# GpSimd's slot scatters of a two-layer attention and experts kernel, moved behind the transposed scores

## The chip, the cores and the metric

The kernel runs on one core of a Trainium2 chip, as one program. A core has four engines that compute, each with its own stream of instructions: TensorE (PE, matrix multiplication), VectorE (DVE), ScalarE (ACT) and GpSimd (POOL), and a fifth, SyncE (SP), that issues DMA transfers. They meet through semaphores alone. The metric is device time in microseconds, the median of several executions. It stands a few microseconds above the span of a profiled execution, which runs from the first to the last instruction.

## The reference

Two layers, each a cross attention and a mixture of eight experts of which every token uses two, on 32 batches of 128 tokens with 256 features. The change lies in the first attention and in what prepares the first experts:

```python
x = x + _L0_xattn_ref(_layernorm(x), ctx_1024, ctx_1024, itok_BxS2_0_31, mask_BxS2_ff1, ...)
    # q = norm(x) @ Wq.T, k = ctx @ Wk.T, v = ctx @ Wv.T, 16 heads of 16
    scores = jnp.einsum('bhqd,bhkd->bhqk', q, k)
    lm = layer_indices[:, :, None] == layer_indices[:, None, :]
    scores = jnp.where(lm, scores + am, NEG)
    attn = jax.nn.softmax(scores, axis=-1)
    ctx = jnp.einsum('bhqk,bhkd->bhqd', attn, v)
    return ctx @ Wo.T + bo
x = x + _L0_ffn_ref(_layernorm(x), router_w, w1, w2, expert_scale)
    logits = xf @ router_w.T
    top_w, top_idx = jax.lax.top_k(jax.nn.softmax(logits), 2)
    # every token goes through its two experts
x = x + _L1_xattn_ref(_layernorm(x), ctx_1024, ...)
x = x + _L1_ffn_ref(_layernorm(x), ...)
```

The kernel computes the experts for the tokens that chose them. So each token gets two slots in a list sorted by expert, and its number is written ("scattered") to these slots in a table in DRAM, from which the experts' stage later reads which rows to gather.

## The kernel before

The program is a row of stages, and each engine runs its part of each stage in order: the first attention (`a_...`), the first experts (`b_...`), the second attention (`c_...`), the second experts (`d_...`). Within a stage nothing is scheduled by a tool. Every engine has one loop over the iterations b, written out by hand, and a block of 128 tokens passes through it over several iterations; `inside(b)` leaves out blocks below 0 and above 31.

In iteration b of the first attention TensorE does, in this order: the scores of block b (L804, tiled matmuls of 32 rows), the values of block b-1 (L843, tiled matmuls of 32 columns), transposes and the term for unseen keys (L932, L863, L872, L852), the router's logits of block b-3 (L941), the transpose of the clamped maxima (L812), the transposed scores (L787, L826 and L830, the last two tiled), the projections of the context of block b+2 (L901, L904), the transpose of `att` (L911), the query projection (L882) and the output projection of block b-1 (L918). VectorE takes the residual and its statistics (L1026 to L1032), the maxima over the scores (L1051), clamps them (`mexp`, L1058), picks experts (L1096, L1098), combines (L1069 to L1076), and for each finished group of blocks makes the slots (L1126 to L1141). ScalarE copies out of PSUM (`oT` L704, `attT` L711 and others) and takes the exponentials (`pT`, L695) of the transposed scores. `st_done[r]`, r from 0 to 3, are the four semaphores that the last transposed scores of a block raise, one for each of four banks of PSUM.

GpSimd's part of an iteration is short. `norm2(b-2)` makes the scale of the second normalisation (L539 to L543, three small instructions that start when VectorE has that block's statistics), `mask(b+1)` compares tokens (L555), `add_bias(b-1)` adds a bias to the residual (L561), and `norm1(b+4)` makes the scale of the first normalisation (L527 to L531). Between them stand the slot scatters. `scatter(b, k)` (L569) is one indirect DMA, which GpSimd issues itself; it writes the numbers of a block's 128 tokens to their slot k, where the slots come from `gsidx`. Two scatters belong to a block. `scattered_at(b, k)` says in which iteration one is issued, and the dictionary `turn` holds the list of each iteration: for the first blocks the two of block b-8 in iteration b, from iteration 8 on, and near the end, where groups get smaller, three in iterations 28 and 29 and four in 30, 31 and 32, then two in each. The first scatter of a group waits for `slot_ready`. When the loop is over, GpSimd waits until all have landed and goes on to the first experts, whose first gathers read the table.

## Time and profile before

| what | us |
| --- | --- |
| runs of the kernel before | 1456.46, 1464.56, 1462.81 |
| their median | 1462.81 |
| span of the profiled execution | 1453.1 |
| TensorE busy in the span | 1337.7 (92%) |
| GpSimd busy in the span | 680.5 (47%) |

A row of a timeline gives the start in us from the span's start, how long the row lasts, the engine, the line, the operation, output and inputs, and how many instructions it merges; in brackets stands how long the engine was idle before it and what ended that. PE is TensorE, DVE VectorE, ACT ScalarE, POOL GpSimd. The granted clock is TensorE's, 1.00 being 2.4 GHz.

### The profile page before, as it was taken

The numbers are of one execution on the slowest core, as the hardware profiler recorded it, in microseconds if no ns is written. First come the engines' busy times: TensorE is split into PE (matmuls) and PEld (weight loads), VectorE is DVE, ScalarE is ACT, GpSimd is POOL, SyncE is SP. The second block draws the span as 40 slices with busy tenths as digits, with TensorE's granted clock in tenths as the row PEclk, the third lists the DMA queues.
The fourth block names the chain that finished last, engine by engine and source line by source line (L and its number), as shares of the span: only waits on it lengthen the run. The fifth ranks groups of instructions, "written<-read, shape, count | busy, mean of one in ns | idle before, by whom it ended". The sixth has DMA issues, their size and how long they took to land.

```text
span 1453.1 us, 37961 instructions
## 1 busy us (share of the span) xinstructions
PE 1337.7 (92%) x13114; PEld 1095.2 (75%) x13114; DVE 866.1 (60%) x2396; ACT 825.9 (57%) x1945; POOL 680.5 (47%) x939
## 2 busy tenths in 40 slices
PE   6999999997779999999997899999974999999997
PEld 5787777775546666666665799999963989889896
DVE  4787777877643333333332688888874666666664
ACT  4787777776345555555553566666643445444443
POOL 4235455455553333333331558778745344444323
PEclk8999999998789999999999899999996999999999
DMA  4344333332159999999996233333213433333331
GB/s 146 95 127 117 101 105 114 99 98 68 34 111 181 204 181 173 178 178 178 178 178 142 77 92 89 91 102 95 88 56 73 128 124 124 126 122 108 121 110 53
DMA packets 280922, 172.99 MB, mean 119 GB/s; under 512 B 213054, under 2 KB 259360, under 8 KB 280740
## 3 DMA queue, kind: packets, MB, share of 16 engines
q1 hardware_dynamic: 259156, 135.85, 39.6%
q0 software_dynamic: 18608, 32.21, 7.9%
q10 hardware_dynamic: 2976, 2.52, 0.6%
q8 instruction: 113, 1.85, 0.6%
q14 instruction: 69, 0.57, 0.2%
HBM read 93.44 MB, written 31.97 MB: 86 GB/s over the span
## 4 chain that ended last, share of the span: by engine, by line
PE 81%; DMA 4%; issue 4%; DVE 4%; ACT 3%; POOL 2%; another core or an unknown queue 1%; SPq 0%; ACTq 0%; DVEq 0%; POOLq 0%
PE psum L2424 14%; PE psum L1495 12%; PE psum L1475 12%; PE psum L2441 7%; PE psum L1996 3%; PE psum L901 2%; PE psum L1986 2%; PE psum L830 2%; PE psum L843 2%; PE psum L804 2%; PE psum L918 2%; PE psum L882 2%; PE psum L904 2%; PE psum L1906 2%; PE psum L1945 2%
## 5 line engine op out<-in xcount | busy, mean ns | idle before, releaser
L2424 PE MATMUL psum<-d_xT,d_w 128*128 128x256 f16 (+1 forms) x2304 | 228.7, 256 | 0.0
L2424 PEld LDWEIGHTS psum<-d_xT,d_w 128*128 128x128 f16 x2304 | 199.3, 98 | 19.0
L1395 DVE SCALAR_TENSOR_TENSOR b_h<-b_hid,b_h 128x1024 f16<-128x1024 f32 x71 | 87.0, 1225 | 211.2 <-ACT b_h L1430 207.9
L1475 PE MATMUL psum<-arena,b_xT 128*128 x852 | 197.2, 382 | 9.6 <-DMA b_xT<-b_x 7.9
L1495 PE MATMUL psum<-arena,b_hT 128*128 x1704 | 197.7, 273 | 3.4 <-DMA b_hT<-b_h 3.4
L1495 PEld LDWEIGHTS psum<-arena,b_hT 128*128 128x128 f16 x1704 | 166.0, 98 | 39.1 <-issue 5.7
L1305 POOL DMA_INDIRECT b_xg<-dram_normed,b_gi x71 | 69.6, 981 | 200.7 <-issue 128.3
L1475 PEld LDWEIGHTS psum<-arena,b_xT 128*128 128x128 f16 x852 | 83.7, 98 | 98.5 <-issue 14.8
L2505 ACT ACTIVATE d_sg<-psum 128x256 f32<-128x256 f32 (+1 forms) x192 | 66.0, 348 | 146.6 <-PE psum L2424 136.5
L2566 DVE SCALAR_TENSOR_TENSOR d_hf<-psum,d_sg 128x256 f32<-128x256 f32 (+1 forms) x192 | 71.1, 379 | 104.0 <-ACT d_sg L2505 85.9
L1423 ACT ACTIVATE b_hid<-psum 128x512 f32<-128x512 f32 x142 | 83.6, 596 | 67.5 <-PE psum L1475 59.6
L2441 PE MATMUL psum<-d_w,d_h 128*128 128x256 f16 x960 | 116.2, 273 | 5.2 <-DVE d_h L2577 2.7
L695 ACT ACTIVATE pT<-psum,amc 128x512 f32<-128x512 f32 x128 | 77.6, 689 | 53.8 <-PE psum L830 46.3
L2441 PEld LDWEIGHTS psum<-d_w,d_h 128*128 128x128 f16 x960 | 90.9, 98 | 16.6 <-issue 3.6
L1051 DVE TENSOR_REDUCE mx<-psum 128x4 f32<-128x512 f32 x128 | 79.5, 683 | 18.3 <-PE psum L804 17.8
L2381 POOL DMA_INDIRECT d_rowsum<-out,d_gi x40 | 43.8, 1096 | 92.2 <-PE psum L2424 67.9
L1716 POOL DMA_INDIRECT c_yg<-dram_expert_rows,c_gi x64 | 66.0, 1031 | 44.2 <-DMA dram_expert_rows<-b_ys 29.3
L2386 POOL DMA_INDIRECT out<-d_rowsum,d_gi x40 | 42.3, 1058 | 88.1 <-DVE d_rowsum L2580 80.2
L1295 POOL DMA_INDIRECT b_gi<-dram_ids,ypos x71 | 69.1, 973 | 27.5 <-issue 23.6
L1414 ACT ACTIVATE b_x<-b_xg 128x256 f16<-128x256 f32 x71 | 29.4, 414 | 92.0 <-DMA b_xg<-dram_normed,b_gi 92.0
L1430 ACT ACTIVATE b_h<-b_hid 128x1024 f16<-128x1024 f32 x71 | 75.0, 1057 | 2.5 <-DMA b_hT<-b_h 0.3
L1749 POOL DMA_INDIRECT dram_ids<-c_gsidw,c_gsidx x64 | 68.1, 1064 | 17.4 <-issue 17.4
(328 smaller groups left out, 3014.7 us busy)
## 6 DMA issues: line engine op xcount, KB each, us to landing
d_wst<-in_L_w SPq DMA_DIRECT2D x64, 384.0 KB
stage<-in_L_w SPq DMA_DIRECT2D x32, 512.0 KB
dram_expert_rows<-b_ys SPq DMA_DIRECT2D x71, 128.0 KB
ctxT<-in_ctxT SPq DMA_DIRECT2D x64, 128.0 KB
dram_normed<-xn SPq DMA_DIRECT2D x64, 128.0 KB
x<-in_x SPq DMA_DIRECT2D x32, 128.0 KB, 5.1
dram_x<-xnew SPq DMA_DIRECT2D x32, 128.0 KB
c_x<-dram_x SPq DMA_DIRECT2D x32, 128.0 KB
```

The source lines that it names most:

```text
L695: act.activation(pT[:, r, :, :].rearrange("p j q -> p (j q)"), psum[:, SB + r, :], ACT.Exp, bias=amc[:, b:b + 1]).then_inc(exp_done[r], 1)
L1051: i = dve.tensor_reduce(mx[:, r, :], psum[:, SB + r, :].rearrange("p (j k) -> p j k", j=HB), AX.X, ALU.max)
L1295: pool.indirect_dma_start(gi[:, j % NX, :], None, ids[0], bass.IndirectOffsetOnAxis(ap=ypos[:, j:j + 1], axis=0)).then_inc(i_ld[j % NX], 16)
L1305: pool.indirect_dma_start(xg[:, j % NX, :], None, xs[0], bass.IndirectOffsetOnAxis(ap=gi[:, j % NX, 0:1], axis=0)).then_inc(g_ld[j % NX], 16)
L1395: dve.scalar_tensor_tensor(out=h16[:, p, 1, :], in0=hid[:, p, :], scalar=H_SCALE, in1=h16[:, p, 0, :], op0=ALU.mult, op1=ALU.subtract).the ...
L1423: act.activation(hid[:, p, half * 512:(half + 1) * 512], psum[:, 1 + 2 * p + half, :], ACT.Silu, scale=1.0 / (X_SCALE * W_SCALE)).then_inc ...
L1430: act.activation(h16[:, p, 0, :], hid[:, p, :], ACT.Copy, scale=H_SCALE).then_inc(hi_done, 1)
L1475: i = pe.matmul(psum[:, 1 + 2 * p + half, :], xT[:, j % NT, px, c, :], weights(e, c, pw, half * 512, 512), start=(n == 0), stop=(n == len( ...
L1495: i = pe.matmul(psum[:, 6 + p, 0:D], hT[:, p, ph_, c, :], weights(e, 2 + c // 4, pw, (c % 4) * D, D), start=(n == 0), stop=(n == len(terms ...
L2424: i = pe.matmul(psum[:, q, m * n:(m + 1) * n], w16[:, fc % RING, pw, col:col + P], xT[:, p, px, c, at:at + n], start=(k == 0), stop=(k == ...
L2441: i = pe.matmul(psum[:, NQ + k, 0:D], h16[:, fc % 2, ph_, k * P:(k + 1) * P], w16[:, fc % RING, pw, 2 * DC * P:UW], start=(fc == 0 and t = ...
L2566: dve.scalar_tensor_tensor(out=hf[:, fc % 2, at:at + n], in0=psum[:, q, n:2 * n], scalar=H_SCALE / (X_SCALE * W_SCALE), in1=sg[:, fc % 2, ...
```

## The change

Before, an iteration's scatters stood in three places on GpSimd: the first behind `mask`, the middle ones (if there are more than two) behind `add_bias`, the last one behind `norm1`. Now all stand together behind `add_bias` and ahead of `norm1`. In iterations of a block inside the range that have scatters (8 to 31), GpSimd first waits until `st_done[3]` of the same iteration's block is raised. Number, targets and contents of the scatters stay the same.

```diff
                     norm2(b - 2)
                     if b > 0:
                         mask(b + 1)
-                    for c in turn.get(b, ())[0:1]:
-                        scatter(*c)
                     add_bias(b - 1)
-                    for c in turn.get(b, ())[1:-1]:
+                    if inside(b) and b in turn:
+                        pool.wait_ge(st_done[NR - 1], b + 1)
+                    for c in turn.get(b, ()):
                         scatter(*c)
                     norm1(b + 4)
-                    for c in turn.get(b, ())[1:][-1:]:
-                        scatter(*c)
```

On GpSimd, one full iteration with two scatters of the kernel before, L539 being the start of `norm2`, L555 `mask`, L561 `add_bias`, L527 the start of `norm1` and L569 a scatter:

```order
L539 TENSOR_SCALAR rstd_69<-mv_68 128x1 [waits xn2_ready,n2_stat]
L541 TENSOR_TENSOR rstd_69<-rstd_69,minus_half 128x1 [waits n2_rstd]
L543 TENSOR_SCALAR rstd_69<-mv_68,rstd_69 128x1 [waits n2_rstd]
L555 TENSOR_SCALAR other<-tokr,tokc 128x128 [waits u_done,neg_ready,col_ready,mask_ld_p1]
L569 DMA dram_ids<-pairs,gsidx 34560x2
L561 TENSOR_TENSOR x_116<-x_116,bob 128x256 [waits xn_ready]
L527 TENSOR_SCALAR rstd_66<-mv_65 128x1 [waits xn_ready,n1_stat]
L529 TENSOR_TENSOR rstd_66<-rstd_66,minus_half 128x1 [waits n1_rstd]
L531 TENSOR_SCALAR rstd_66<-mv_65,rstd_66 128x1 [waits n1_rstd]
L569 DMA dram_ids<-pairs,gsidx 34560x2
```

and the same iteration of the changed kernel:

```order
L539 TENSOR_SCALAR rstd_69<-mv_68 128x1 [waits xn2_ready,n2_stat]
L541 TENSOR_TENSOR rstd_69<-rstd_69,minus_half 128x1 [waits n2_rstd]
L543 TENSOR_SCALAR rstd_69<-mv_68,rstd_69 128x1 [waits n2_rstd]
L555 TENSOR_SCALAR other<-tokr,tokc 128x128 [waits u_done,neg_ready,col_ready,mask_ld_p1]
L561 TENSOR_TENSOR x_116<-x_116,bob 128x256 [waits xn_ready]
L569 DMA dram_ids<-pairs,gsidx 34560x2 [waits st_done3]
L569 DMA dram_ids<-pairs,gsidx 34560x2
L527 TENSOR_SCALAR rstd_66<-mv_65 128x1 [waits xn_ready,n1_stat]
L529 TENSOR_TENSOR rstd_66<-rstd_66,minus_half 128x1 [waits n1_rstd]
L531 TENSOR_SCALAR rstd_66<-mv_65,rstd_66 128x1 [waits n1_rstd]
```

One scatter moved down past `add_bias`, the other up past `norm1`, and the first of them now waits for the transposed scores.

On GpSimd in iteration 30, which has four scatters and no `norm1`, before:

```order
L555 TENSOR_SCALAR other<-tokr,tokc 128x128 [waits u_done,neg_ready,col_ready,mask_ld_p1]
L569 DMA dram_ids<-pairs,gsidx 34560x2
L561 TENSOR_TENSOR x_116<-x_116,bob 128x256 [waits xn_ready]
L569 DMA dram_ids<-pairs,gsidx 34560x2
L569 DMA dram_ids<-pairs,gsidx 34560x2 [waits slot_ready]
L569 DMA dram_ids<-pairs,gsidx 34560x2
```

and now:

```order
L555 TENSOR_SCALAR other<-tokr,tokc 128x128 [waits u_done,neg_ready,col_ready,mask_ld_p1]
L561 TENSOR_TENSOR x_116<-x_116,bob 128x256 [waits xn_ready]
L569 DMA dram_ids<-pairs,gsidx 34560x2 [waits st_done3]
L569 DMA dram_ids<-pairs,gsidx 34560x2
L569 DMA dram_ids<-pairs,gsidx 34560x2 [waits slot_ready]
L569 DMA dram_ids<-pairs,gsidx 34560x2
```

All four follow each other, behind the wait. No other engine's instructions change their order.

## Rows read from the trace of the kernel before

**Rows 1.** The page: the span, and the chain that ended last, by engine.

```profile
span 1453.1 us, 37961 instructions
...
PE 81%; DMA 4%; issue 4%; DVE 4%; ACT 3%; POOL 2%; another core or an unknown queue 1%; SPq 0%; ACTq 0%; DVEq 0%; POOLq 0%
```

**Rows 2.** Busy time by stretch; iterations 3-7, 8-27, 28, 29, 30; columns in the first.

```profile
core 0: us, PE busy (x) PEld busy (x) DVE busy (x) ACT busy (x) POOL busy (x), PEclk, DMA share, GB/s
53.46:105.06 51.60, 50.89 (x738) 41.29 (x738) 41.02 (x118) 41.76 (x103) 16.50 (x37) 1.00 0.37 115
105.06:325.44 220.38, 210.29 (x2945) 169.30 (x2945) 174.32 (x521) 169.18 (x411) 114.36 (x199) 0.98 0.39 108
325.44:338.19 12.75, 11.75 (x149) 9.44 (x149) 8.97 (x30) 8.65 (x23) 7.73 (x12) 0.87 0.37 79
338.19:350.40 12.21, 10.65 (x153) 8.47 (x153) 9.04 (x29) 8.37 (x23) 5.58 (x8) 1.00 0.32 67
350.40:365.00 14.60, 8.59 (x126) 5.92 (x127) 9.12 (x29) 7.22 (x17) 6.57 (x9) 0.80 0.15 52
```

**Rows 3.** Timeline of iteration 5, from 74.07: VectorE, then ScalarE and TensorE.

```profile
75.44 2.48 DVE L1051 TENSOR_REDUCE mx<-psum 128x4 f32<-128x512 f32 x4 [0.17 <-PE psum L804]
77.96 0.23 DVE L1058 TENSOR_SCALAR mexp<-mx,negrow 128x16 f16<-128x16 f32 x1
...
80.54 2.42 ACT L695 ACTIVATE pT<-psum,amc 128x512 f32<-128x512 f32 x4 [1.42 <-PE psum L830]
82.84 0.40 ACT L711 ACTIVATE attT<-psum 128x256 f32<-128x256 f32 x1
...
82.30 0.38 PE L911 MATMUL psum<-ident,att 128*128 128x128 f32 x2
...
83.41 1.03 PE L918 MATMUL psum<-wo,attT 128*128 128x256 f32 x4
```

**Rows 4.** Timeline of iteration 10: GpSimd's first scatter and VectorE's clamp.

```profile
130.22 1.08 POOL L569 DMA_INDIRECT dram_ids<-pairs,gsidx  x1 [0.17 <-issue]
...
130.67 0.67 DVE L1058 TENSOR_SCALAR mexp<-mx,negrow 128x16 f16<-128x16 f32 x1
```

**Rows 5.** VectorE by line, 105 to 325: busy us, mean ns of one, idle before.

```profile
L1058 DVE TENSOR_SCALAR mexp<-mx,negrow 128x16 f16<-128x16 f32 x20 | 8.8, 441 | 0.7
```

**Rows 6.** Timeline of iteration 17: a scatter, TensorE's scores, VectorE's maxima.

```profile
204.93 1.08 POOL L569 DMA_INDIRECT dram_ids<-pairs,gsidx  x1 [0.16 <-issue]
...
204.38 1.06 PE L804 MATMUL psum<-kT,qeo 32*128 32x128 f32 x32
...
206.43 2.48 DVE L1051 TENSOR_REDUCE mx<-psum 128x4 f32<-128x512 f32 x4 [1.06 <-PE psum L804]
```

**Rows 7.** Timeline of iteration 16: a scatter, TensorE's values, ScalarE's copy of them.

```profile
194.72 1.08 POOL L569 DMA_INDIRECT dram_ids<-pairs,gsidx  x1 [0.16 <-issue]
...
194.24 1.08 PE L843 MATMUL psum<-pT,v 128*32 128x128 f32 x32
...
196.45 0.60 ACT L704 ACTIVATE oT<-psum 128x512 f32<-128x512 f32 x1 [1.30 <-PE psum L843]
```

**Rows 8.** Timeline of iterations 29 and 30: last scatter of 29, exponentials of both.

```profile
344.96 0.97 POOL L569 DMA_INDIRECT dram_ids<-pairs,gsidx  x1 [0.30 <-issue]
...
346.58 2.42 ACT L695 ACTIVATE pT<-psum,amc 128x512 f32<-128x512 f32 x4 [3.02 <-remote]
...
360.24 2.42 ACT L695 ACTIVATE pT<-psum,amc 128x512 f32<-128x512 f32 x4 [4.48 <-remote]
```

**Rows 9.** Timeline around 161: output projection, a scatter, VectorE's residual.

```profile
160.01 1.03 PE L918 MATMUL psum<-wo,attT 128*128 128x256 f32 x4
...
160.13 1.08 POOL L569 DMA_INDIRECT dram_ids<-pairs,gsidx  x1 [0.16 <-issue]
...
161.08 0.42 DVE L1026 TENSOR_TENSOR xnew<-psum,x 128x256 f32<-128x256 f32 x1 [2.47 <-ACT xn L726]
```

**Rows 10.** Busy time by stretch, columns as in rows 2: within iteration 12.

```profile
154.30:157.60 3.30, 3.30 (x33) 2.65 (x25) 3.06 (x13) 1.19 (x3) 0.76 (x2) 0.53 0.02 3
```

## The prediction

> **What bounds the kernel now.** I read the page first: the chain that ended last is TensorE for 81% of a span of 1453.1 us [rows 1]. So the first attention stage costs what its iterations last, and what the change can give is TensorE time lost there. The second view is the busy time by stretch [rows 2]; each stretch begins where an iteration begins. Iterations 3 to 7 carry no slot scatter and last 51.60 / 5 = 10.32 us each, with TensorE busy for 50.89 of 51.60 us at a granted clock of 1.00. They are the floor: the same work with nothing in its way. Iterations 8 to 27 carry the scatters, about two each, and last 220.38 / 20 = 11.02 us, TensorE busy for 210.29 us, clock 0.98. Then come 12.75, 12.21 and 14.60 us for iterations 28, 29 and 30. Iterations 6 and 7 also carry the routing work of a group (experts' choice, count, slots), so that work is in the floor and does not explain the difference.
>
> The third view is the timeline, engine by engine. [Rows 3] is iteration 5 (from 74.07), undisturbed: VectorE idles 0.17 us between the scores and its maxima, the clamp of the maxima (`mexp`) takes 0.23 us, the exponentials start at 80.54, 6.47 us in, and the end is a tight chain: transpose of `att` until 82.68, copy `attT` 82.84 to 83.24, output projection from 83.41.
>
> **What a scatter does now, by its place.** Three effects, each with a case.
> (a) A scatter starts at 130.22 and ends at 131.30; the clamp, begun at 130.67, lasts until 131.34, 0.67 us instead of 0.23, with TensorE's transpose behind it [rows 4]. Over the 20 iterations the clamp's mean is 441 ns [rows 5]: 20 x 0.21 = 4.2 us.
> (b) A scatter over the end of the scores. They end at 205.44, the maxima start at 206.43, 0.42 us after the scatter's end at 206.01 [rows 6]: idle 1.06 us instead of 0.17. Likewise the values end at 195.32 and ScalarE's copy starts at 196.45, 0.65 us after the scatter's end at 195.80 [rows 7].
> (c) Scatters in a row over the end of the transposed scores. In iteration 29 (from 338.19) the exponentials start at 346.58, 8.39 us in and 0.65 us after the last scatter's end; in iteration 30 (from 350.40) at 360.24, 9.84 us in [rows 8].
> So a signal that leaves one of TensorE's tiled matmuls (32 rows or columns) while a scatter runs is seen 0.4 to 0.65 us after the scatter's end. That of a full 128x128 matmul is not held: the output projection ends at 161.04, inside the scatter of 160.13 to 161.21, and the residual starts at 161.08 [rows 9]. And the clock adds to it: behind TensorE's waits in iteration 12 it falls to 0.53 between 154.3 and 157.6 [rows 10], for the most part the 1.2 GHz level; iteration 28 has 0.87 [rows 2].
>
> **The change, part by part.** *The order*: one iteration's scatters now stand behind `add_bias` and ahead of `norm1`, on GpSimd alone. *The wait* is for the transposed scores of the same iteration, so in iteration 5's times the scatters would start 0.2 us after 80.54. Two take 1.08 + 0.30 + 0.97 = 2.35 us by [rows 4, 8], so until 83.1. Behind the waiting instruction stand `norm1(b+4)` and the next iteration's `norm2` and `mask`. `norm1` feeds a normalisation of ScalarE one iteration later; `norm2` needs a residual that VectorE makes only when the next scores have begun. Both have room, and GpSimd idles there, so I cost the wait at nothing; with that room gone it would cost a scatter's 1 us per iteration.
> *What the scatters now lie beside.* The clamp, the scores and the values are over: (a) and (b) go. The signals of the transposed scores have left: (c) goes. From 80.7 to 83.1 TensorE runs full matmuls, and the next tiled signal is that of the next scores. The one signal that someone waits for closely is the `att` transpose's at 82.68, inside the second scatter. By [rows 9] it passes; the other value is rival 2.
>
> *The sum*, against the profiled execution:
> - iterations 8 to 27: 220.38 - 20 x 10.32 = 14.0 us go, the clock's share among them, since TensorE then has the load of iterations 3 to 7, at which the clock held 1.00;
> - iteration 28: 12.75 - 10.32 = 2.4 us;
> - iteration 29: exponentials 8.39 - 6.47 = 1.9 us late, which goes;
> - iteration 30: 9.84 - 6.47 = 3.4 us. That leaves 11.2 of its 14.60 us; TensorE still idles there for want of later blocks, so I leave the cost of its slow clock (0.80) in;
> - given back: iteration 30 has four scatters, 4 x 1.27 = 5.1 us from 6.7 us on, which reach over the end of the next scores: one hold, 0.5 us.
> Sum 14.0 + 2.4 + 1.9 + 3.4 - 0.5 = 21.2 us. Behind iteration 31 the last scatters wait for slots that VectorE makes block by block, which the change doesn't touch: nothing there. Later stages only start sooner. The span becomes 1453.1 - 21.2 = 1431.9 us; the runs shown lie 3 to 11 us above the span, their median is 1462.8, and I forecast 1462.8 - 21.2 = **1441.6 us**. Bounds: with the full clock in iterations 30 and 31 up to 3 us more go; if a quarter of the holds only moves, 5 us less.
>
> **A rule against the rows.** By [rows 4] the clamp ends with the scatter; by [rows 6 to 8] signals are late as well. The Trainium skill, "SBUF — State Buffer", section "Who interferes with whom", has VectorE and GpSimd share a port pair under an exclusive lock that a `tensor_scalar` can take, and says that TensorE and ScalarE never wait on anyone. The clamp agrees with that; the late signals lie outside it.
>
> **Rivals.**
> 1. *Only the clamp is freed*, and the late signals come from something else, or the holds fall on other signals of the same worth. Then 4.2 us and twice 0.44 for iterations 29 and 30 go: 5 us, 1458 us. For it: the late engines' operands have nothing to do with a scatter. Against it: each of the late starts sits 0.42 to 0.65 us behind a scatter's end, and [rows 3] has none. The skill's rule, taken alone, forecasts the same.
> 2. *The `att` transpose's signal is held too.* The second scatter ends at 83.1; with 0.65 the copy starts at 83.75 instead of 82.84 and the projection at 84.2 instead of 83.41: 0.75 us in each of 20 iterations, 15 us back, 1456.6 us. For it: the signal leaves in the middle of a scatter. Against it: [rows 9].
> 3. *Slower: the scatters hold the exponentials.* The wait names one of four signals of the transposed scores. If the first scatter begins before ScalarE has seen all four, the exponentials start as in iteration 29, 0.65 us behind the pair's end: 83.75 instead of 80.54, 3.2 us in each of 23 iterations, 74 us on top of the forecast, 1515 us. What decides is whether the last of the four reaches ScalarE before the scatter, whose issue alone takes 0.2 us. For it: iteration 29, where the signals left 0.3 us behind one scatter and just ahead of another. Against it: here none runs ahead of them.
> 4. *It doesn't do what it says*, as the wait was met long before. The order shows it on the signal of the same iteration, for which GpSimd, idle, really waits; no time of its own.
>
> **How the numbers follow.** Forecast 0.73, its own range 1436 to 1447; rival 1 0.09; rival 2 0.09; rival 3 0.05; something unlooked for 0.04. The range goes from 1435 to 1457 and takes in rival 2; it leaves out rivals 1 and 3. A measurement of this kernel can tell about 0.5% from no change, 7.3 us, so faster means below 1455.5. Faster: the forecast, a third of rival 2 and half of the unlooked for, 0.78. Within: the rest of rival 2 and rival 1, 0.15. Slower: 0.07.
>
> **What would show it.** Right: iterations 8 to 28 start every 10.3 to 10.4 us; the clamp's mean is 0.23 us again; the maxima follow their scores after 0.17 us idle; the scatters lie 6.7 to 9.0 us into an iteration; the exponentials start 6.5 us in, also in iterations 29 and 30; clock 1.00 up to iteration 29. Wrong: ScalarE waits for the transpose of `att` (rival 2), exponentials at 9.7 us into an iteration (rival 3), iterations still near 11 us with other waits ahead of TensorE (rival 1).

## The result and the profile after

| kernel | runs, us | median |
| --- | --- | --- |
| before | 1456.46, 1464.56, 1462.81, 1464.62 | 1463.68 |
| changed | 1439.36, 1444.17, 1438.76, 1435.53 | 1439.06 |

The ratio is 0.9855, 95% interval 0.9832 to 0.9878: the changed kernel is 1.5% faster. The forecast was 1441.6 us, the measured median is 1439.1, inside the range. Later series ran on four other chips, each beside the kernel before, and where the changed kernel itself was among them (chip C) the change was worth about a seventh of that, too little to tell from nothing by the times. Most of what follows is about this difference. I call the chip of this first comparison A and the others B to E. Which piece of silicon A is was not recorded. It may even be one of the other four, so A stands for a chip or for its circumstances at the time.

The page after, to set against [rows 1], has a span of 1437.1 us, 16.0 less than 1453.1:

```profile
span 1437.1 us, 37967 instructions
...
PE 77%; DVE 7%; issue 6%; ACT 4%; DMA 3%; POOL 2%; another core or an unknown queue 0%; ACTq 0%; SPq 0%; DVEq 0%; POOLq 0%
```

The whole runs differ by 24.6 us at the median, the two profiled ones by 17.1 (1456.46 and 1439.36), because the profiled execution of before was the fastest of its four. Busy time by stretch, as in [rows 2]: iterations 3 to 7, 8 to 27, then 28, 29 and 30.

```profile
core 0: us, PE busy (x) PEld busy (x) DVE busy (x) ACT busy (x) POOL busy (x), PEclk, DMA share, GB/s
54.35:105.95 51.60, 50.90 (x738) 41.31 (x738) 41.00 (x118) 41.71 (x103) 16.44 (x37) 1.00 0.38 115
105.95:313.64 207.69, 204.31 (x2942) 165.42 (x2943) 172.29 (x521) 167.99 (x411) 123.75 (x200) 1.00 0.49 113
313.64:324.08 10.44, 10.20 (x148) 8.22 (x148) 9.17 (x31) 8.51 (x22) 6.36 (x11) 1.00 0.55 106
324.08:335.00 10.92, 10.64 (x153) 8.57 (x153) 8.63 (x29) 8.63 (x23) 5.51 (x9) 1.00 0.54 78
335.00:345.17 10.17, 7.66 (x126) 5.42 (x127) 8.68 (x29) 7.19 (x17) 6.14 (x9) 1.00 0.23 77
```

Iterations 3 to 7 are as before. Iterations 8 to 27 take 207.69 us instead of 220.38, and the granted clock is 1.00 in all of them. A stretch of iteration 17 (from 199.59), engine by engine, answers to [rows 3] and [rows 6]:

```profile
200.97 0.69 DVE L1049 TENSOR_REDUCE mx<-psum 128x4 f32<-128x512 f32 x1 [0.18 <-PE psum L802]
...
203.48 0.23 DVE L1056 TENSOR_SCALAR mexp<-mx,negrow 128x16 f16<-128x16 f32 x1
...
206.06 0.69 ACT L693 ACTIVATE pT<-psum,amc 128x512 f32<-128x512 f32 x1 [1.43 <-PE psum L828]
...
206.44 2.14 POOL L569 DMA_INDIRECT dram_ids<-pairs,gsidx  x1 [2.92 <-PE psum L828]
208.89 0.97 POOL L569 DMA_INDIRECT dram_ids<-pairs,gsidx  x1 [0.30 <-issue]
...
206.41 1.22 DVE L1080 SCALAR_TENSOR_TENSOR arena<-stage,arena 128x1024 f16<-128x1024 f32 x1
```

The maxima follow the scores after 0.18 us idle (1.06 in [rows 6]). The clamp takes 0.23 us. The exponentials start 6.47 us into the iteration, exactly as in iteration 5 of before. The scatters lie behind them. One thing is new: the first scatter lasts 2.14 us. It begins 0.03 us behind the start of VectorE's scaling of a weight tile. By line, over iterations 8 to 27, with mean ns behind the busy time:

```profile
L569 POOL DMA_INDIRECT dram_ids<-pairs,gsidx x40 | 53.1, 1326 | 63.9 <-PE psum L828 57.8 <-issue 6.1
...
L1056 DVE TENSOR_SCALAR mexp<-mx,negrow 128x16 f16<-128x16 f32 x20 | 5.8, 288 | 0.7
```

The clamp's mean is 288 ns against 441 in [rows 5], and not 230. The rest comes from every fourth iteration, where GpSimd's `add_bias` comes late and lies beside it (iteration 16):

```profile
192.77 0.73 POOL L561 TENSOR_TENSOR x<-x,bob 128x256 f32<-128x256 f32 x1
...
193.04 0.50 DVE L1056 TENSOR_SCALAR mexp<-mx,negrow 128x16 f16<-128x16 f32 x1
```

Late signals are not quite gone. At the end of iteration 28 its third scatter starts at 323.30 and ends at 324.27; the output projection ends at 324.14, and the residual starts at 325.04, 0.90 us later. That is what makes iteration 29 last 10.92 us, and its exponentials start 7.1 us in.

```profile
323.30 0.97 POOL L569 DMA_INDIRECT dram_ids<-pairs,gsidx  x1 [0.30 <-issue]
...
323.11 1.03 PE L916 MATMUL psum<-wo,attT 128*128 128x256 f32 x4
...
325.04 0.42 DVE L1024 TENSOR_TENSOR xnew<-psum,x 128x256 f32<-128x256 f32 x1 [1.71 <-PE psum L916]
```

In iteration 30 the exponentials start at 341.35, 6.35 us in, where [rows 8] have 9.84; the scatters begin 0.39 us behind them:

```profile
341.35 2.42 ACT L693 ACTIVATE pT<-psum,amc 128x512 f32<-128x512 f32 x4 [1.43 <-PE psum L828]
...
341.74 1.08 POOL L569 DMA_INDIRECT dram_ids<-pairs,gsidx  x1 [2.78 <-PE psum L828]
```

The last of iteration 30's four scatters reaches over the end of the next scores (346.45), as the prediction had it, and the maxima start 1.0 us behind its end, after 1.36 us idle:

```profile
345.76 0.97 POOL L569 DMA_INDIRECT dram_ids<-pairs,gsidx  x1 [0.31 <-issue]
...
347.74 1.29 DVE L1049 TENSOR_REDUCE mx<-psum 128x4 f32<-128x512 f32 x2 [1.36 <-PE psum L802]
```

### The profile page after: what moved, and what is told of

It is laid out like the page before. It is cut to its first block, busy times and chain, and to the rows that moved or that the text cites. A ratio compares the mean times of both kernels' runs of the same rounds, so it can differ in the third digit from the quotient of the medians.

```text
span 1437.1 us, 37967 instructions
## 1 busy us (share of the span) xinstructions
PE 1331.6 (93%) x13114; PEld 1089.8 (76%) x13114; DVE 862.4 (60%) x2396; ACT 823.1 (57%) x1945; POOL 686.1 (48%) x939
## 4 chain that ended last, share of the span: by engine, by line
PE 77%; DVE 7%; issue 6%; ACT 4%; DMA 3%; POOL 2%; another core or an unknown queue 0%; ACTq 0%; SPq 0%; DVEq 0%; POOLq 0%
PE psum L2422 15%; PE psum L1473 12%; PE psum L1493 12%; PE psum L2439 7%; PE psum L1994 3%; PE psum L1984 2%; PE psum L899 2%; PE psum L1943 2%; PE psum L1904 2%; PE psum L828 2%; PE psum L1910 2%; PE psum L902 2%; DVE mx L1049 2%; PE psum L880 2%; PE psum L841 1%
## 5 line engine op out<-in xcount | busy, mean ns | idle before, releaser
L569 POOL DMA_INDIRECT dram_ids<-pairs,gsidx x64 | 78.5, 1226 | 83.5 <-PE psum L828 70.2
```

The source lines that it names most:

```text
L569: pool.indirect_dma_start(ids[0], bass.IndirectOffsetOnAxis(ap=gsidx[:, g % 4, at:at + 1], axis=0), pairs[:, b, :], None, bounds_check=bou ...
```

## The experiments

My theory was the prediction's: a signal of TensorE that leaves while a scatter runs is seen late, and so is the clamp held; the change takes both away. The rival was that only the clamp counts. The first series should tell them apart by the place of the scatters. It ran on chip B, beside the kernel before, which took 1430.02 us there at the median of 31 runs (1421.99 to 1436.23). That alone was a surprise: 34 us less than on chip A.

### The order without the wait (e1, chip B)

```diff
                     add_bias(b - 1)
-                    if inside(b) and b in turn:
-                        pool.wait_ge(st_done[NR - 1], b + 1)
                     for c in turn.get(b, ()):
```

> The changed kernel without its new wait: an iteration's scatters stand together behind add_bias and start as soon as that is done, some 3.9 us into an iteration. Theory (a tiled matmul's signal that leaves during a scatter is seen only about 0.65 us after its end): the second scatter lies over the end of the transposed scores, 6.2 us into the iteration, the exponentials start 0.6 to 0.7 us late, iterations 8 to 27 last about 10.9 us, and 28 to 30, with three or four scatters in a row, 12 us and more, as in the kernel before: 1455 to 1464 us, no difference from before that can be told. Rival (the order alone does it, since it takes the scatter away from the clamp, and only the clamp counts): iterations 8 to 27 at 10.4 us, 1440 us, the same as the changed kernel.

Measured: 1426.64 us, ratio 0.997 (0.9951 to 0.999). Iterations 8 to 27:

```profile
108.85:316.44 207.59, 204.31 (x2943) 165.44 (x2944) 172.62 (x521) 167.93 (x411) 112.31 (x200) 1.00 0.43 114
```

10.38 us per iteration, as the rival had it, though the second scatter does lie over the end of the transposed scores. In iteration 17 it runs from 207.96 to 208.93, the transposed scores end at 208.90, and the exponentials start at 208.93, on time.

### The wait without the order (e2, chip B)

```diff
                         mask(b + 1)
+                    if inside(b) and b in turn:
+                        pool.wait_ge(st_done[NR - 1], b + 1)
                     for c in turn.get(b, ())[0:1]:
                         scatter(*c)
                     add_bias(b - 1)
```

> The kernel before with the new wait alone: the scatters keep their places (behind mask, behind add_bias, behind norm1), but the first one waits for the transposed scores. Theory (what counts is only which signals a scatter lies over): the first scatter lies at 6.8 to 7.9 us, the second behind norm1 at about 9.8 to 10.9, so add_bias moves away from the clamp too; the exponentials start 6.5 us in; iterations 8 to 27 at 10.3 to 10.45 us, 1436 to 1444 us. The second scatter may now lie over the end of the next iteration's first matmuls; if it holds one of their signals, 0.4 us per iteration more, 1448 us. Rival (that they run together is what gains): half of the gain or less, 1450 us or more.

Measured: 1427.70 us, ratio 0.9981 (0.9966 to 0.9996). Iterations 8 to 27, and the clamp in them:

```profile
106.69:314.86 208.17, 204.81 (x2943) 165.07 (x2943) 174.53 (x521) 168.28 (x409) 128.55 (x199) 1.00 0.48 113
...
L1060 DVE TENSOR_SCALAR mexp<-mx,negrow 128x16 f16<-128x16 f32 x20 | 4.7, 235 | 0.7
```

The clamp is wholly free, 235 ns, since `add_bias` moved too. For the clamp togetherness isn't needed; the place is what counts. The second scatter lies later than I expected, mostly 0.8 to 1.9 us into the next iteration and over the end of its scores, and nothing starts late behind it.

### The first scatter stays (e3, chip B)

```diff
                         mask(b + 1)
+                    for c in turn.get(b, ())[0:1]:
+                        scatter(*c)
                     add_bias(b - 1)
                     if inside(b) and b in turn:
                         pool.wait_ge(st_done[NR - 1], b + 1)
-                    for c in turn.get(b, ()):
+                    for c in turn.get(b, ())[1:]:
                         scatter(*c)
```

> The changed kernel with an iteration's first scatter put back to its old place, behind mask; the others stay behind add_bias and the wait. Theory: the first scatter lies over the clamp again, which lasts 0.44 to 0.67 us on the mean instead of 0.29, and in some iterations over the end of the scores or values: 0.2 to 0.4 us per iteration, iterations 8 to 27 at 10.6 to 10.75 us, 1444 to 1448 us in all. Rival (the scatters in the exponentials' way were the whole loss, the clamp has slack behind it): 1439 to 1441 us, iterations at 10.4 us.

Measured: 1429.77 us, ratio 0.9993 (0.9977 to 1.0008), the only one of this series whose interval holds 1. Iterations 8 to 27, and the clamp in them:

```profile
108.73:320.35 211.62, 205.25 (x2945) 165.73 (x2945) 177.05 (x521) 169.00 (x411) 117.76 (x200) 1.00 0.47 111
...
L1058 DVE TENSOR_SCALAR mexp<-mx,negrow 128x16 f16<-128x16 f32 x20 | 11.9, 594 | 0.7
```

The clamp has little slack: its mean is 0.31 us above e4's 282 ns, 6.2 us in 20 iterations, and the stretch is 4.0 us longer than e4's. So about two thirds of what the clamp loses reaches the stage, and the rival, that the clamp has slack behind it, is out.

### The wait two steps earlier (e4, chip B)

```diff
                     if inside(b) and b in turn:
-                        pool.wait_ge(st_done[NR - 1], b + 1)
+                        pool.wait_ge(mt_done, b + 1)
```

> The changed kernel with the wait set on the transposed maxima (about 4.3 us into an iteration) instead of the transposed scores: the same order, the same number of waits, but the pair now lies at about 4.6 to 6.9 us, over the end of the transposed scores in every iteration. Theory: the exponentials start about 0.65 us behind the pair's end, 7.5 us into the iteration instead of 6.5; iterations 8 to 27 last 11.0 to 11.6 us, and the clock falls below 1.00 in some: 1455 to 1475 us. Rival (only the clamp and the port that VectorE and GpSimd share count): the pair is clear of the clamp, so 1438 to 1442 us, exponentials 6.5 us in.

Measured: 1427.33 us, ratio 0.9969 (0.9946 to 0.9992), where the theory wanted 1455 or more. Iterations 8 to 27, and iteration 17's second scatter, transposed scores and exponentials:

```profile
108.11:315.72 207.61, 204.31 (x2944) 165.40 (x2944) 171.82 (x521) 168.18 (x411) 113.24 (x200) 1.00 0.47 113
...
207.82 1.08 POOL L569 DMA_INDIRECT dram_ids<-pairs,gsidx  x1 [0.31 <-issue]
...
207.08 1.08 PE L828 MATMUL psum<-qeo,kT 32*128 32x256 f32 x13
...
208.19 0.69 ACT L693 ACTIVATE pT<-psum,amc 128x512 f32<-128x512 f32 x1 [1.42 <-PE psum L828]
```

The transposed scores end at 208.16, 0.34 us into the scatter, and ScalarE starts 0.03 us later, with 0.7 us of the scatter still to run. It is so in every iteration from 9 to 30 of this trace: the transposed scores end inside a scatter and none of their signals is held. Either the moved scatters no longer do it, or this chip never did it. So the two kernels themselves had to be traced away from chip A.

### Both kernels again (b1 and a1, chip C)

> The kernel before, unchanged, once more, for its trace beside the experiments: beside them it took 1430 us at the median, 33 us less than the 1462.8 us from which the prediction started. Theory (the late signals of TensorE behind a scatter belong to the chip or to the circumstances of an execution, not to the program): where it runs in 1430 us, its trace shows no signal of TensorE seen late in a scatter; the maxima follow the scores after 0.1 to 0.2 us, the exponentials start 6.5 us into an iteration, and the one cost left is the clamp under a scatter: iterations 8 to 27 at 10.55 to 10.65 us, 211 to 213 us in all instead of 220.4, iterations 28 to 30 at 10.3 to 10.7 us. Rival (the stage costs the same as before, and the 33 us come from the later stages): iterations 8 to 27 at 11.0 us again, with exponentials at 8.4 and 9.8 us in iterations 29 and 30.

> The changed kernel, unchanged, once more, beside the kernel before on the chip of this series. Theory: if the late signals are there (the kernel before at 1455 us and more), it is faster by 20 to 25 us, ratio 0.983 to 0.988; if they are not (the kernel before at about 1430 us), all that it can give is the clamp's 4 to 5 us and what the clock makes of them, ratio 0.996 to 0.999, about 1426 us, iterations 8 to 27 at 10.38 us. Rival (the change gives its 24 us everywhere): ratio 0.983 to 0.988 also where the kernel before takes 1430 us.

Measured: before 1430.75 us at the median of 13 runs (the traced one, b1, 1428.79), changed 1427.32 (10 runs), ratio 0.9988 (0.9965 to 1.0011). Iterations 8 to 27 and 28 to 30 of before, the clamp in the first of these, and iteration 11's scatter, scores and maxima:

```profile
104.91:315.55 210.64, 205.31 (x2945) 165.81 (x2945) 180.14 (x521) 168.32 (x411) 114.25 (x199) 1.00 0.43 112
315.55:347.07 31.52, 28.20 (x420) 22.04 (x420) 27.60 (x88) 24.11 (x60) 20.02 (x29) 1.00 0.34 83
...
L1058 DVE TENSOR_SCALAR mexp<-mx,negrow 128x16 f16<-128x16 f32 x20 | 10.4, 522 | 0.7
...
136.70 1.08 POOL L569 DMA_INDIRECT dram_ids<-pairs,gsidx  x1 [0.16 <-issue]
...
136.58 1.06 PE L804 MATMUL psum<-kT,qeo 32*128 32x128 f32 x32
...
137.74 1.89 DVE L1051 TENSOR_REDUCE mx<-psum 128x4 f32<-128x512 f32 x3 [0.17 <-PE psum L804]
```

The same program, the same scatter over the end of the same scores as in [rows 6]: there the maxima started 0.42 us behind the scatter's end after 1.06 us idle, here they start after 0.17 us, while the scatter still runs (until 137.78). What is left of the cost is the clamp. The same stretches of the changed kernel:

```profile
104.09:311.83 207.74, 204.30 (x2943) 165.41 (x2944) 172.37 (x520) 168.02 (x411) 122.69 (x200) 1.00 0.50 113
311.83:342.75 30.92, 28.09 (x420) 21.96 (x421) 26.49 (x89) 24.22 (x60) 18.30 (x27) 1.00 0.46 89
```

210.64 - 207.74 = 2.9 us and 31.52 - 30.92 = 0.6 us: the change gives 3.5 us on chip C, 0.2% of the kernel, which the timed ratio can't tell from nothing and doesn't contradict. On chip A it gave 12.7 and 8.0 us. The changed kernel's iterations 8 to 27 take the same on both (207.69 and 207.74); the kernels before differ. At the end of iteration 28, where chip A held the residual, it isn't held here; the third scatter runs until 322.45, and the residual starts at 322.37:

```profile
321.48 0.97 POOL L569 DMA_INDIRECT dram_ids<-pairs,gsidx  x1 [0.30 <-issue]
...
322.37 0.42 DVE L1024 TENSOR_TENSOR xnew<-psum,x 128x256 f32<-128x256 f32 x1 [0.85 <-PE psum L916]
```

The late signals of chip A aren't confined to this stage. Of the second attention, which the change doesn't touch, first the whole stage and a copy of ScalarE by line (idle before it, and by whom) of the changed kernel on chip A:

```profile
795.90:1076.90 281.00, 259.58 (x2352) 247.30 (x2352) 223.18 (x852) 166.24 (x533) 193.25 (x296) 0.99 0.30 86
...
L1809 ACT ACTIVATE c_tcT<-psum,c_bm 128x128 f32<-128x128 f32 x64 | 20.0, 365 | 14.3 <-PE psum L1943 11.7 <-DMA tokr<-dram_tokens 2.6
```

and then on chip C:

```profile
790.90:1066.00 275.10, 260.06 (x2352) 246.59 (x2352) 224.91 (x852) 171.01 (x533) 194.95 (x296) 0.99 0.32 88
...
L1809 ACT ACTIVATE c_tcT<-psum,c_bm 128x128 f32<-128x128 f32 x64 | 20.0, 363 | 1.7 <-PE psum L1943 1.3
```

The same copies stand idle for 14.3 us on A, most of it for TensorE's signals, and for 1.7 on C, and the stage is 5.9 us longer. I also counted, in every trace from 50 us on, the starts of VectorE and ScalarE that follow an idle time of theirs and whose last signal is TensorE's as the profile infers it, 530 to 595 in each. More than 0.35 us behind that matmul's end came 66 in the kernel before and 55 in the changed one on chip A, 48 and 38 of these with the matmul's end inside one of GpSimd's indirect DMAs. In each of the 12 traces from chips B to E there are 3 to 6, nearly all at the same places of the program, at most 3 of them inside an indirect DMA.

The traces also hold the time of each semaphore's update, which the lines above don't print, and it shows where the delay lies. In [rows 6] the scores end at 205.44, the first of their four semaphores is raised only at 206.33, and VectorE starts 0.10 us later: the signal is late, not the engine that waits for it. The scores, the values and the transposed scores raise four semaphores each, almost at once. Up to iteration 30, 56 of these updates fall due inside a scatter in the kernel before on chip A: 52 come 0.50 to 1.01 us late, 2 within 0.17 us, and 2 aren't on record. In b1 there are 79, all within 0.18 us.

### Five places in one kernel (e7 on chip C, e8 on chip D)

```diff
-                        pool.wait_ge(st_done[NR - 1], b + 1)
+                        at = b % 5 if 8 <= b < 28 else 4
+                        pool.wait_ge(*((s_done[NR - 1], b + 1), (pv_done[0], b), (mt_done, b + 1),
+                                       (kv_done, b + 3), (st_done[NR - 1], b + 1))[at])
```

> The changed kernel with five places for the pair of scatters, in turn, iteration by iteration, by another signal to wait for in iterations 8 to 27: iteration number modulo 5 equal to 0: the end of the scores (the pair lies at about 1.5 to 3.8 us, or behind add_bias at 3.9 to 6.2 us if that is later); 1: the values of the block before (the same bound); 2: the transposed maxima (4.6 to 6.9); 3: the end of the key and value projection, where TensorE is further on (about 8.4 to 10.7); 4: the transposed scores, as the change has it (6.8 to 9.1). Theory, where TensorE's signals are seen late in a scatter: iterations with remainder 0 to 2 show the exponentials 0.6 to 1.3 us late and last 10.9 to 11.6 us, those with remainder 3 show the next scores' maxima or the projection's residual late by 0.4 to 1 us, and those with remainder 4 last 10.3 to 10.5 us. Theory, where they are not: every iteration lasts 10.3 to 10.65 us wherever the pair lies, with no start more than 0.3 us behind the signal of TensorE that it waits for. Rival (the place within the iteration matters in itself): the iterations differ by their remainder even where no signal is seen late.

> The five places for the pair of scatters once more (the remainder of the iteration number modulo 5 chooses, as before), on whichever chip this series gets, for the late signals have shown on one chip and not on two others. Theory, if this chip shows late signals (the kernel before at 1455 us and more beside it): iterations with remainder 0 to 2 have the exponentials 0.6 to 1.3 us late and last 10.9 to 11.6 us, those with remainder 4 last 10.3 to 10.5 us. If it does not (the kernel before at 1425 to 1435 us): every iteration lasts 10.3 to 10.65 us, as on the chip of the run before. Rival (the absence of late signals in the first sweep came from the sweep's own program): iterations of 11 us with remainders 0 to 2 although the kernel before takes 1430 us.

Measured: 1433.84 us (e7, one run; the kernel before 1430.75) and 1426.00 us (e8, one run; the kernel before 1429.41). Iterations 8 to 27 of e7:

```profile
105.63:313.18 207.55, 204.24 (x2944) 165.41 (x2945) 172.19 (x521) 168.12 (x411) 116.11 (x200) 1.00 0.47 114
```

and 207.67 us in e8. Remainders 0 and 1 both put the pair behind `add_bias`, at about 4.1 to 6.8 us, so the five waits make four places. The place makes no difference on these chips: iterations 15 to 19, one for each remainder in turn, last 10.38, 10.38, 10.30, 10.31 and 10.37 us in e7, and 10.37, 10.42, 10.30, 10.31 and 10.37 in the kernel without scatters, which comes next.

### No scatters (e5, chip D)

```diff
-                    pool.indirect_dma_start(ids[0], bass.IndirectOffsetOnAxis(ap=gsidx[:, g % 4, at:at + 1], axis=0),
-                                            pairs[:, b, :], None, bounds_check=bound, oob_is_err=False).then_inc(scat[g % 4], 16)
+                    pass
...
-                for p in range(4):
-                    pool.wait_ge(scat[p], scattered(len(GROUPS) - 1, p))
...
-                    if due(g - 3):
-                        dve.wait_ge(scat[g % 4], scattered(g - 4, g % 4))
```

> The changed kernel without the first attention stage's slot scatters and without the waits for them (that part is left out: no token slots are written, so the later experts gather the zero row). It gives the floor of the stage. Theory: iterations 8 to 27 take 206.3 us (10.31 each), as in iterations 3 to 7, plus what add_bias costs under the clamp in every fourth iteration (0.05 to 0.1 us each time) and what the group routing costs; so the scatters of the changed kernel, 207.7 us for these iterations, cost at most 1.4 us in all. Rival (the scatters still cost something where they now lie): 204 us or less, more than 3 us below the changed kernel.

Measured: 1431.60 us (one run; the kernel before 1429.41). Since its experts gather other rows, only this stage is compared. Iterations 8 to 27:

```profile
106.16:313.91 207.75, 204.32 (x2944) 165.42 (x2944) 171.90 (x521) 168.07 (x411) 70.15 (x160) 1.00 0.39 114
```

That is the changed kernel's time on A (207.69) and on C (207.74). So where the scatters now lie they cost nothing, and the floor of these iterations is 10.39 us, not 10.32. I had put it at 206.3 us; the other 1.4 us are for the most part in iterations 9, 11, 27 and the multiples of four, the clamp beside `add_bias` among them (its mean is 290 ns here too).

### GpSimd busy without a DMA (e6, chip E)

```diff
+                def busy():
+                    pool.tensor_tensor(junk[:, :], junk[:, :], junk[:, :], ALU.add)
...
                         mask(b + 1)
+                    if b in turn and b < 25:
+                        busy()
                     add_bias(b - 1)
...
                         scatter(*c)
+                    if b in turn and b < 25:
+                        busy()
                     norm1(b + 4)
```

> The changed kernel with two additions of GpSimd that nothing else uses, SBUF to SBUF on 128x352, about 1 us each and without any DMA, at the scatters' old places (behind mask and behind add_bias) in iterations 8 to 24 that carry scatters. Theory (the clamp is held by GpSimd's work as such, not by the transfer of a scatter): the clamp, which begins 3.89 us into an iteration, lasts until the first addition ends, 0.45 to 0.8 us, so those iterations last 10.5 to 10.8 us against 10.3 in iterations 25 and 26; no signal of TensorE is seen late. Rival (only an indirect DMA holds it): clamp 0.23 us, 10.3 to 10.4 us per iteration.

The edit puts the second addition behind `norm1`, and not behind `add_bias` as the expectation says; the first one, behind `mask`, is the one that meets the clamp. Measured: 1434.82 us (one run; the kernel before 1436.66). Iterations 8 to 27, the clamp in them, and iteration 22's addition and clamp:

```profile
106.86:318.91 212.05, 204.92 (x2945) 165.49 (x2945) 176.23 (x521) 168.75 (x411) 148.38 (x234) 1.00 0.50 111
...
L1065 DVE TENSOR_SCALAR mexp<-mx,negrow 128x16 f16<-128x16 f32 x20 | 10.5, 524 | 0.7
...
259.23 0.77 POOL L591 TENSOR_TENSOR junk<-junk 128x352 f32<-128x352 f32 x1
...
259.23 0.80 DVE L1065 TENSOR_SCALAR mexp<-mx,negrow 128x16 f16<-128x16 f32 x1
```

The clamp lasts until GpSimd's addition has ended, though nothing is transferred: it is GpSimd's work that holds it, a scatter's or a plain addition's. The Trainium skill, "SBUF — State Buffer", section "Who interferes with whom", says that VectorE in a mode that takes the port pair shared with GpSimd and an instruction of GpSimd block each other fully, and that the one issued first has the pair to its end; the rows agree with it, though no view shows the clamp's mode. One thing stays unexplained: once, in iteration 18, ScalarE's copy of the values starts 1.06 us behind their end (1.32 us idle). No scatter is near it. The four semaphores of the values are raised 0.77 to 0.88 us late there, as on chip A, so late signals are confined neither to chip A nor to scatters.

### The order alone and the earlier wait again (e9 and e10, chip E)

The edits are those of e1 and e4. They were to meet the late signals, should they show again.

> The changed kernel without its wait once more, on whichever chip this series gets. If this chip shows late signals (the kernel before at 1455 us and more beside it): theory: second scatter over the end of the transposed scores, exponentials 0.6 to 0.7 us late, iterations 8 to 27 at 10.9 us, 28 to 30 at 12 us and more, 1450 to 1464 us in all; rival: as the changed kernel, 1440 us. If it does not (the kernel before at 1425 to 1435 us): iterations 8 to 27 at 10.4 us and the exponentials on time, as on the first chip that this kernel ran on, and the two do not differ.

> The changed kernel with its wait set on the transposed maxima once more, on whichever chip this series gets. If this chip shows late signals (the kernel before at 1455 us and more beside it): theory: the exponentials start 7.5 us into an iteration, iterations at 11.0 to 11.6 us, 1455 to 1475 us in all; rival: as the changed kernel. If it does not: iterations at 10.3 to 10.65 us, 1422 to 1434 us, no difference from the changed kernel.

Measured: 1422.06 and 1429.21 us (one run each; the kernel before 1436.66). Iterations 8 to 27 take 207.64 and 207.60 us: no late signals in these two either, and in this stage both are as good as the change. They told nothing new about chip A.

### The stage on each chip

| kernel | chip | iterations 8 to 27, us | 28 to 30, us | clamp, mean ns |
| --- | --- | --- | --- | --- |
| before | A | 220.38 | 39.56 | 441 |
| changed | A | 207.69 | 31.53 | 288 |
| before | C | 210.64 | 31.52 | 522 |
| changed | C | 207.74 | 30.92 | 290 |
| e3, first scatter stays | B | 211.62 | 31.52 | 594 |
| e6, GpSimd busy | E | 212.05 | 30.92 | 524 |
| e5, no scatters | D | 207.75 | 31.59 | 290 |
| e1, e9, order alone | B, E | 207.59, 207.64 | 31.83, 31.48 | 282, 284 |
| e2, wait alone | B | 208.17 | 31.94 | 235 |
| e4, e10, earlier wait | B, E | 207.61, 207.60 | 31.80, 31.81 | 282, 281 |
| e7, e8, five places | C, D | 207.55, 207.67 | 31.81, 31.49 | 275, 280 |

Most variants stand 0.6 to 1.0 us above 30.92 in iterations 28 to 30. Except in e3, where the clamp is held there too, this is the clock's doing and not the scatters'. Iteration 30 lasts 11.17 us at a granted clock of 0.90 in e1 and 11.11 at 0.91 in e7, where its scatters stand as in the changed kernel; in the changed kernel it lasts 10.17 at 1.00 on both A and C, and without any scatter (e5) the three take 31.59. Before and changed on chip C, both at 1.00, can be set against each other.

## Why the prediction came out right, and what was wrong in it

**The sum.** Against the profiled execution of before, on chip A:

| term | forecast, us | measured, us |
| --- | --- | --- |
| iterations 8 to 27 | 14.0 | 220.38 - 207.69 = 12.7 |
| iteration 28 | 2.4 | 12.75 - 10.44 = 2.3 |
| iteration 29 | 1.9 | 12.21 - 10.92 = 1.3 |
| iteration 30 | 3.4 | 14.60 - 10.17 = 4.4 |
| given back | -0.5 | behind iteration 30, not in this sum |
| sum | 21.2 | 20.7 |

- *Iterations 8 to 27* were over-sized by 1.3 us through the floor. The prediction held the routing work to be in iterations 3 to 7 already, but iterations 9, 11 and 27 last 10.5 to 10.65 us without scatters too (e5), so 10.39 and not 10.32 us was to be had. The gain itself was all of what there was.
- *Iteration 29* lost 0.6 us to a late signal of the output projection. The prediction held this very signal to be safe. It had the cost of one hold, 0.5 us, on the next scores behind iteration 30; that hold came as well (the maxima at 347.74), and lies behind the iterations of this sum.
- *Iteration 30* gave 1.0 us more, because the clock, 0.80 before, stayed at 1.00. I had left the clock's share in and given it as a bound. This much is luck: e7, with the same scatters there, had 0.91 and 11.11 us.
- The span fell by 16.0 and not 20.7 us: in the changed kernel's execution the stage starts 0.9 us later, and the stages behind iteration 30 take 3.8 us more in sum. On chip C the later stages of the two kernels do not differ in that direction (the second attention 275.0 and 275.1 us), so I take this for the spread of executions; no run settles it.

**The steps that held, on chip A.** Iterations 8 to 28 are 10.3 to 10.65 us long, the maxima 0.18 us behind the scores, the exponentials 6.47 us in and 6.35 in iteration 30 (7.1 in iteration 29, behind the late projection), the clock 1.00. The clamp's mean fell to 288 ns and not to the forecast 230, for `add_bias` lies beside it in every fourth iteration. The wait costs nothing in iterations 8 to 27, for the changed kernel isn't slower there than the one without scatters. Rival 3 did not occur: the first scatter starts 0.38 us behind the exponentials, not ahead of them. Rival 2 did not occur either: in each of iterations 8 to 29 the transposes of `att` end inside a scatter, and the copy `attT` starts 0.16 us behind them each time, as without one. The fourth rival is out by the idle time "[2.92 <-PE psum L828]" of GpSimd.

**The steps that failed.** The prediction read the late signals as a property of this program: whatever tiled matmul signals during a scatter is seen late. That is true, nearly without exception, of the two traces of chip A and of none of the twelve from chips B to E, the kernel before itself among them (b1). So the number came out right because the result was measured where the trace had been taken. On chip C the same forecast of 21 us would have been wrong by 18.

The prediction's own case (c) already went beyond its rule. In iterations 29 and 30 of the kernel before the transposed scores end at 344.95 and 357.14, in the short gaps between two scatters (344.65 to 344.96, 356.87 to 357.18), and their signals are held all the same, the second one for 3.1 us and over two scatters. Its exponentials start 0.81 us behind the last scatter's end (359.43), and not within the 0.42 to 0.65 us that the prediction gives for all.

The distinction between tiled and full 128x128 matmuls, on which rival 2's small chance rested, falls on chip A as well: the output projection, a full one, is seen 0.90 us late. The trace of the kernel before had such a case in the second attention, where the prediction didn't look. The matmuls of L1945 end at 870.81, inside a scatter, and ScalarE starts 0.92 us later:

```profile
870.36 1.18 POOL L1749 DMA_INDIRECT dram_ids<-c_gsidw,c_gsidx  x1 [0.30 <-issue]
...
869.98 0.83 PE L1945 MATMUL psum<-c_x,c_Wk_s 128*128 128x128 f16 x12
...
871.73 0.63 ACT L1811 ACTIVATE c_tcT<-psum,c_bm 128x128 f32<-128x128 f32 x2 [1.17 <-PE psum L1945]
```

In the first attention, signals that come four at once are held nearly always and single ones mostly pass, but I have no rule that tells which single ones don't. Off chip A the kernel follows rival 1, "only the clamp is freed", with its price: forecast 5 us, measured 3.5 us on chip C. The Trainium skill's sentence beside it in the prediction ("SBUF — State Buffer", section "Who interferes with whom": TensorE and ScalarE never wait on anyone) is about ports. The traces of chips B to E agree with it but for the one case in e6; on chip A, ScalarE and VectorE start late because TensorE's signals come late.

The scatters' own length was mis-sized too: 1.08 and 0.97 us forecast, 1.33 us on the mean now, up to 2.14. VectorE's `SCALAR_TENSOR_TENSOR` with two inputs in SBUF begins just before, and the scatter lasts until 0.95 us behind its end (206.41 + 1.22 = 207.63; 206.44 + 2.14 = 208.58). Twenty scatters of iterations 8 to 27 begin within such an instruction; 17 of them end 0.84 to 0.97 us behind its end, and three, which begin closest behind its start (0.02 to 0.03 us), take 0.97 us as if it weren't there. It costs nothing here, since nobody waits for GpSimd.

**What stays open.** Why signals are late on chip A. It isn't the program, since b1 is the same program. It isn't one odd execution, since the four runs of before lie within 1456 to 1465 us. Whether it is the silicon or something that ran beside it, no run tells. One rival wasn't tested: that the late signals come with the recording of the profile. The two traces of chip A hold 17888 and 18007 updates of semaphores, the twelve others 22546 to 23670, and in iterations 3 to 7, which have no scatters, none is missing in either. Every execution on record has a span and a clock from the profiler, so no run shows what chip A does without it. Nor was any variant seen on chip A, so whether the wait is needed there in addition to the order is argued from [rows 8], not shown. The change doesn't make up for all of chip A either: the changed kernel takes 1439.1 us there and 1427.3 on C. Off chip A the wait costs nothing that the times show, and of the versions tried the changed kernel is the only one seen to be good on both A and another chip. The ratios of e1, e2 and e4 to the kernel before (0.997, 0.9981, 0.9969) all lie within the changed kernel's interval on C (0.9965 to 1.0011).

## What to carry to other kernels

Issue GpSimd's indirect DMAs where no short VectorE instruction and no closely awaited matmul is due, even if a wait has to be added for it: here that was free on both chips that ran it, A and C, and took iterations 8 to 27 down to the time they have with no scatters at all (207.7 us each). Away from the clamp is what the runs show everywhere; away from the matmuls' signals counted on chip A alone. Before a gain read from one trace is credited to a program, run the unchanged kernel on another chip: the same edit was worth 20.7 us of the stage on one and 3.5 on another. And take the floor of a stretch from that stretch with the suspected work left out, not from neighbouring iterations, which gave 1.4 us too little.

## What the hardware showed that I had not expected

- In one of the five sets of runs (A), VectorE and ScalarE start 0.4 to 1.4 us late behind many matmuls, mostly those that end within an indirect DMA of GpSimd, and once 3.1 us late; where an update is on record, it is the signal itself that is late. The kernel before takes 34 us longer there (1463.7 against 1430), 17.8 of them in this stage's iterations 8 to 30 ([rows 2], 259.94 us, against 210.64 + 31.52 = 242.16) and 5.0 us in the second attention (280.0 against 275.0 from its first matmul to its last). The rest wasn't followed up.
- A clamp of 128x16 values, 0.23 us alone, takes until the end of what GpSimd has begun: 0.80 us beside a mere addition of 0.77 us (e6), up to 0.79 us beside a scatter (e3).
- The blocking goes both ways: a scatter of 1.08 us becomes 2.14 when it begins 0.03 to 0.04 us behind a VectorE instruction of 1.22 us with two inputs in SBUF. Closer still, it can pass unhurt: begun 0.02 us behind one, it took 0.97 us (iteration 15).
